# Two transfers of destination rows per visit in place of five, in a two-layer graph network on one Trainium2 core

## What is computed

```python
# layer 0
q, k, v = feat @ Wq.T + bq, feat @ Wk.T + bk, feat @ Wv.T + bv      # (n, 8, 32)
score = clip(einsum('ehd,ehd->eh', q[edge_dst], k[edge_src]) / sqrt(32), -10, 10)
alpha = softmax of score over the edges of one destination
wv = segment_sum(alpha * v[edge_src], edge_dst)
x = feat + wv @ Wp.T + bp;  x = x + gelu(layernorm(x) @ W1.T + b1) @ W2.T + b2
# layer 1
z = leaky_relu((feature @ W_s.T)[src] + (feature @ W_t.T)[dst], 0.2)
e = z @ W_attn.T;  alpha = softmax of e over the edges of one source
out = segment_sum(feature[src] * alpha, dst) @ W_fc.T + b_fc
# each layer is followed by x = layernorm(x + layer(x))
```

## Time and profile before

| | us |
|---|---|
| median of the three runs | 4053.36 |
| the profiled execution, its time | 4052.72 |
| the profiled execution, its span | 4050.9 |
| pass 0 (attention of layer 0) | from 155 to 1560 |
| feed-forward part and projections | 1560 to 1950 |
| pass 1 (scores of layer 1) | 1950 to 3215 |
| softmax sums | 3215 to 3370 |
| third pass (sums of layer 1) | 3370 to 4050 |

### The profile page before, as it was taken

One profiled execution on the slowest core, in us unless ns is written; L12 is line 12 of the kernel. 1 busy time (PEld: TensorE's weight loads), 2 busy tenths in 40 slices (PEclk: granted clock), 3 DMA queues, 4 the chain that ended last, 5 costly groups with the idle time before them and its releaser, 6 DMA issues. The chain is left out here.

```text
span 4050.9 us, 56408 instructions
## 1 busy us (share of the span) xinstructions
PE 2350.9 (58%) x11454; PEld 1705.1 (42%) x11455; DVE 2223.8 (55%) x6089; ACT 1218.1 (30%) x3239; POOL 1941.0 (48%) x1970
## 2 busy tenths in 40 slices
PE   4666666666666665887333333333333396777776
PEld 2344444444444444675122222222222195566555
DVE  5565565555555563334344444444444596677675
ACT  0255555555555553333122222222222200111111
POOL 0255555555555552212655656655555303444443
PEclk9888888888888887898565666666666656888998
DMA  4666665665666662113667677666766605666664
GB/s 140 196 175 176 176 177 174 180 181 169 177 178 179 176 182 84 65 63 100 207 205 205 206 210 209 200 202 203 205 200 200 181 0 164 200 205 198 193 208 148
DMA packets 365706, 698.61 MB, mean 172 GB/s; under 512 B 77317, under 2 KB 247039, under 8 KB 365674
## 3 DMA queue, kind: packets, MB, share of 16 engines
q0 software_dynamic: 134784, 425.63, 36.1%
q1 hardware_dynamic: 220602, 256.40, 20.2%
q10 hardware_dynamic: 10288, 16.23, 1.1%
HBM read 597.23 MB, written 100.85 MB: 172 GB/s over the span
## 5 line engine op out<-in xcount | busy, mean ns | idle before, releaser
L878 PE MATMUL ps_px<-sb_parts,sb_bits 128*128 x4860 | 886.7, 344 | 902.9 <-DVEq L1590 362.3
L759 POOL DMA_INDIRECT sb_ring<-kv_rows,sb_idx x810 | 792.3, 978 | 723.8 <-DVE sb_msg L1458 377.5
L878 PEld LDWEIGHTS ps_px<-sb_parts,sb_bits 128*128 128x128 bf16 x4860 | 566.5, 121 | 1238.4 <-DVEq L1590 586.7
L888 PE MATMUL ps_pa<-sb_msg,sb_onehot 128*128 128x264 f32 x1620 | 567.5, 483 | 433.1 <-DVE sb_msg L1458 349.0
L1125 ACT ACTIVATE sb_bits<-sb_bits 128x256 bf16<-128x256 bf16 x810 | 322.7, 409 | 1019.2 <-remote 725.9
L1443 DVE TENSOR_TENSOR sb_prod<-ps_px,sb_ring 128x512 f32<-128x512 f32 x405 | 278.7, 688 | 573.7 <-remote 339.9
L888 PEld LDWEIGHTS ps_pa<-sb_msg,sb_onehot 128*128 128x128 f32 x1620 | 345.0, 235 | 551.3 <-DVE sb_msg L1458 373.6
L759 POOL DMA_INDIRECT sb_ring<-proj_rows,sb_idx x324 | 311.7, 962 | 321.8 <-issue 156.1
L759 POOL DMA_INDIRECT sb_w<-narrow_rows,sb_idx x324 | 310.1, 957 | 207.4 <-DVEq L1590 113.0
L759 POOL DMA_INDIRECT sb_w<-feat_rows,sb_idx x162 | 158.6, 979 | 426.1 <-issue 190.3
L1593 DVE SCALAR_TENSOR_TENSOR sb_prod<-sb_msg,sb_attn_hi 128x256 f32<-128x256 f32 x810 | 300.5, 421 | 0.7 <-issue 0.7
(11 more groups left out here) (242 smaller groups left out, 3070.2 us busy)
## 6 DMA issues: line engine op xcount, KB each, us to landing
sb_bits<-dst_short SPq DMA_DIRECT2D x280, 192.0 KB
x_edges<-sb_ring SPq DMA_DIRECT2D x54, 768.0 KB
sb_slots<-x_edges SPq DMA_DIRECT2D x54, 768.0 KB
x_edges<-sb_slots SPq DMA_DIRECT2D x27, 768.0 KB
sb_w<-x_edges SPq DMA_DIRECT2D x27, 768.0 KB
sb_msg<-lo_rows SPq DMA_DIRECT2D x28, 576.0 KB
sb_ring<-kv_rows,sb_idx POOLq DMA_INDIRECT x810
kv_rows<-sb_slots ACTq DMA_DIRECT2D x25, 256.0 KB, 2.8
```

What stands on the lines that cost most here:

```text
L759: pool.indirect_dma_start(out=out[:, i, :], out_offset=None, in_=rows, in_offset=bass.IndirectOffsetOnAxis(ap=idx[:, 2 * p + i:2 * p + i + ...
L878: mm = pe.matmul(px[:, j, 0:width], onehot_t[:, j, :], flat(visit_parts[:, bass.ds(parity, 1), a, 0:width]), start=(a == 0), stop=(a == 2))
L888: mm = pe.matmul(pa[:, 0:C + H], onehot[:, j, :], msg[:, j, :], start=(p == 0 and i == 0), stop=True, skip_group_check=True)
```

## The change

The destinations of a visit come in two transfers: halves 0 to 2 in one of 4608 bytes per partition, halves 3 and 4 in one of 3072 bytes. The first is issued after ACT has read half 2, the second after half 4. Each has its own semaphore; ACT waits for the first before halves 0 to 2 and for the second before halves 3 and 4. `node_parts` loads the whole rows of 774 bf16 elements (1548 bytes), also in pass 0, in both passes as one contiguous run per node.

```diff
-        drow_in = [[sem(f"drow_in{L}_{h}") for h in range(HALVES)] for L in range(2)]
+        drow_in = [[sem(f"drow_in{L}_{g}") for g in range(2)] for L in range(2)]
...
+        ROW_HALVES = [[0, 1, 2], [3, 4]]
...
-                width = CW if L else C
...
-                def rows(tile, h):
-                    sp.dma_start(drow[:, h].rearrange("p j e -> p (j e)"),
-                                 dst_short[bass.ds(tile + h * R, R), :].rearrange("j e -> (j e)").partition_broadcast(P)).then_inc(drow_in[L][h], 16)
+                def rows(tile, g):
+                    h, n = ROW_HALVES[g][0], len(ROW_HALVES[g])
+                    sp.dma_start(drow[:, h:h + n].rearrange("p h j e -> p (h j e)"),
+                                 dst_short[bass.ds(tile + h * R, n * R), :].rearrange("j e -> (j e)").partition_broadcast(P)).then_inc(drow_in[L][g], 16)
 
                 def node_parts(node, parity):
-                    sp.dma_start(visit_parts[:, bass.ds(parity, 1), :, 0:width].rearrange("p o a c -> p (o a) c"),
-                                 part_rows[bass.ds(node, P), :, 0:width]).then_inc(node_in[L], 16)
+                    sp.dma_start(visit_parts[:, bass.ds(parity, 1)].rearrange("p o a c -> p (o a c)"),
+                                 part_rows[bass.ds(node, P)].rearrange("n a c -> n (a c)")).then_inc(node_in[L], 16)
...
-                for h in range(HALVES):
-                    rows(tile, h)
+                for g in range(2):
+                    rows(tile, g)
                 for c in range(THIRDS):
                     indices(tile, c)
...
                         sp.wait_ge(far[L], v * HALVES + h + 2)
                         sp.sem_inc(sp_seen, 1)
-                        rows(after, h)
+                        for g in range(2):
+                            if h == ROW_HALVES[g][-1]:
+                                rows(after, g)
...
-                act.wait_ge(drow_in[L][h], v * 16 + 16)
+                act.wait_ge(drow_in[L][h >= ROW_HALVES[1][0]], v * 16 + 16)
```

More of the change, by code:

```diff
@@ L588, in run @@
                         sp.sem_inc(sp_seen, 1)
-                    for h in range(HALVES):
-                        sp.wait_ge(drow_in[L][h], total * 16 + 16)
+                    for g in range(2):
+                        sp.wait_ge(drow_in[L][g], total * 16 + 16)
                         sp.sem_inc(sp_seen, 1)
```

## The result

The changed kernel takes 4010.35 us (median of five runs, 4004.60 to 4019.04), the kernel before, run beside it, 4053.36 us. The ratio is 0.9893, with a 95% interval from 0.9868 to 0.9918: 43 us less, where 20 were forecast. The profiled executions differ by 42.4 us (4050.9 and 4008.5), and the place of each first and last gather tells where.

A forecast was written before the change was run, and what follows sets the result against it. Waits, not a busy engine, were taken to bound passes 0 and 1, with SP's late index loads in pass 1. Against 4052.72 us, -21 + 7 - 1.6 - 4 = -19.6 gave 4033 us, range 3995 to 4072.

The forecast's parts named there:

- The pause at the first gather: Pass 1, POOL's wait for indices at a visit's start: 1.0 us shorter per visit, from 6.3 to about 5.3 us.
- In 21 visits: Pass 1: the 1.0 us gain counted in 21 visits, 21 us; at most 48 us, at least nothing.
- nothing for the other index loads: Pass 1: removing half 3's load ahead of the second index load, needed for pair 5, is worth nothing; no wait shows.
- a different rhythm of stalls: Pass 1: a stall fewer or more per visit, 4 to 6 us x 26, would upset the forecast altogether.
- The give-back: Pass 1: a third of the gain lost to a longer pause before pair 9, +7 us; between 0 and all 21.
- The seam: Between pass 0 and pass 1: three load issues fewer on SP while POOL stands idle, -1.6 us.
- Packets: Pass 0: fewer and larger packets on the load queue, -4 us, bound 9 us; pass 1: 0.
- Bursts and later loads: Both passes: bunched loads cost 0 (bad end +40 us in pass 1); ACT's waits for later-issued loads stay hidden.
- B: Rival: nothing moves, 4050 us; what SP gains at pair 0 in pass 1 is lost at pair 9; chance 0.20.
- C: Rival: pass 1's first pause falls to that of pair 9, indices issued in loaded time, about 4000 us; chance 0.15.
- D: Rival: bunched loads delay the first gathers after each pause, +40 us over 26 visits, about 4086 us; chance 0.15.
- E: Rival: pass 1's node_parts already went as 128 packets, so only pass 0's cut counts; already in the sum, no own chance.

The follow-up runs named there:

- Experiment 6: The changed kernel with eight semaphore increments that nothing waits for, put on SP ahead of each visit's first index load in pass 1: 4029.38 us, ratio 0.9933.
- Experiment 8: The changed kernel with pass 1's node_parts load issued behind the first index load, the two transfers of destinations behind the second and third: 3995.84 us, ratio 0.9849.
- parts_whole: The kernel before with node_parts loading whole rows in pass 0 as well, the five transfers of destinations kept: 4047.32 us, ratio 0.9986.
- five_late_3: The kernel before with its five 192 KB transfers issued where the changed kernel issues its two (three after half 2, two after half 4): 4014.86 us, ratio 0.9914.
- pass1_only: The kernel before with the change made in pass 1 alone, pass 0 loading as before: 3344.91 us, ratio 0.9989, in a 3344 us session.
- small_slots: The changed kernel with 32 KB row loads after halves 0 and 1, 512 KB after half 2: 1.0006 and 1.0005 in 3344 us sessions, 0.9961 in a slow one.

## Why the prediction was right and wrong

The direction, the place and the range were right. The size was less than half of what came (20 us of 43), by two terms of the sum in pass 1.

**The pause at the first gather, 1.0 us shorter: nearly right.** Forecast were 0.6 us from SP's issue and 0.4 us from the bytes. Measured are 0.69 us (4.28 to 3.59, last gather to issue) and 0.58 us (3.25 to 2.67, issue to start, 0.52 of them in the load's own packets). The forecast pause was 5.3 us; it is 4.97, where it was 6.36.

**"In 21 visits", and nothing for the other index loads: this step failed.** I multiplied a shorter pause by an unchanged number of pauses at the first gather, 21 us, with 48 as the upper bound. There the number fell to 9 and the sum by 98.7 us (147.7 - 49.0). But I had also set the load ahead of the second index load at nothing, since no wait for it showed. After the change POOL waits 15 times, 57.3 us, for the second and third index load, before it 2 times, 7.9 us. All three loads together, the waits over 2 us fell from 153.9 us in 26 to 101.0 us in 24: 53 us, by their length and not by their number. Experiment 6 shows that 0.3 us on SP's queue move the number at the first gather by about ten. I had named "a different rhythm of stalls" as what would upset the forecast, and gave it no term.

**The give-back, a third: failed too, in size and in kind.** It is 63 of 99 us, the other pauses' growth from 134.4 to 197.2. I had DVE a pair behind and a longer pause before pair 9; there the pauses fell from 21 to 8. Of the 63 us, 49 are the waits for the second and third index load, 5 are waits over 2 us for slots (102.8 to 108.1), and the rest is in pauses under 2 us. The net is 36 us, forecast 14. Experiment 8, in which each load of rows is issued right behind an index load, is without most of these waits and takes 19.5 us less in pass 1.

**The seam, -1.6 us: not seen.** It is 353.8 and 354.3 us in the two, and 351.6 in `parts_whole`, which has all eight issues there; what differs from run to run is larger than the term.

**Packets, -4 us in pass 0: the size was off.** Measured are 7.5 us, near the bound of 9, and all of it from `node_parts`. My way to it, engine time per byte, was wrong or at least unproven, since that time hardly changed.

**Bursts and later loads, 0: nothing speaks against it.** ACT waits for no load of destinations in pass 1, and `five_late_3` and the changed kernel, the one with five small and the other with two large transfers at the same places, have pass 1 within 7.2 us of one another. The size of the packets is tested by that; the bunching, which both have, is not tested by itself.

**The rivals.** B, nothing moves, is out. C had the pause fall to that of pair 9, and gave 4000 us; the time comes near to it, but not by its way, since where there is a pause it is still 5 us. Its argument, SP's instructions being so slow in the loaded time that a few fewer are worth much, is what seems to have been weighed too low: eight marks ahead of the index load cost 18 to 21 us. D is out: the 40 us did not come, and packets of 4608 and 3072 bytes do no worse in pass 1 (1257.4 us) than packets of 1536 bytes at the same places (1264.6). The Trainium skill's rule that a DMA engine turns between queues at whole packets ("DMA: Bandwidth & Descriptors", section Queues, rings and completion order) is neither shown nor refuted by that; a harm from it does not show here. E was as told: in the body of pass 1 `node_parts` was already whole.

The 2.67 us from the issue of a 5 KB load to POOL's start contain 0.44 us of packets; the other 2.2 us are not packets (before the change 3.25 less 0.96, 2.3 us). The Trainium skill (same page, section Anatomy of one DMA) has about 2.0 us fixed, and has it for DMAs that GpSimd issues, not for every DMA as the prediction says. These loads, which SP issues, agree with it in size. The 2.2 us are paid on the path only by the loads that are issued late.

## What to carry to other kernels

Where an engine that issues DMAs runs a queue of mixed loads, the load that somebody is about to wait for belongs first, and the others behind it; how many transfers the others are matters less. Before multiplying a shorter wait by its count, ask where the engine will wait next: here most of the waits for the first index load went over to the second and the third, which were hardly waited for before, and a few tenths of a microsecond on the queue changed where the pauses fall. And where a wait has two conditions that come together, time it against the issue and the packets of each instead of trusting the one that the profile names.

## What was not expected of the hardware

**Two speeds of the same program.** The kernel before took 4053 to 4065 us in some sessions and 3343 to 3345 us in others, and nothing in between. Windows of `pass1_only` at 3345 us, pass 0 and pass 1:

```profile
160.00:1300.00 1140.00, 822.21 (x4205) 567.69 (x4206) 818.90 (x1761) 717.79 (x2215) 784.39 (x803) 0.93 0.74 216
1670.00:2670.00 1000.00, 512.71 (x2362) 299.48 (x2360) 605.74 (x2363) 286.09 (x524) 760.16 (x788) 0.62 0.86 259
```

Against the earlier trace rows the engines do the same work; in pass 1 the clock is the same 0.62, and the DMA engines are busy 86% of the time in place of 69%. The other engines don't come to a stop: in pass 1 the longest wait of ACT is 6.7 us and that of DVE 4.4 us, in the kernel before at 4053 us 15.7 and 13.1 us. SP's instructions that only control differ too; whether they are the cause or another sign of it is not shown. The marks at L524 (L526 in `pass1_only`), over 400 us of pass 1, first at 4053 us, then at 3345 us (ns, least, median, most):

```profile
L524 SPq EVENT_SEMAPHORE  x203: 3/17/733, 2206.0 to 2600.0; - x102
```

```profile
L526 SPq EVENT_SEMAPHORE  x248: 17/17/17, 1904.8 to 2291.5; - x124
```

None of 248 takes over 17 ns in the one. In the other 53 of 203 take over 600 ns, some 40 times the median, as those that stand in the loaded time of the earlier trace rows do. At 3345 us SP has time to spare and waits for the gathers to land, which it does nowhere in pass 1 at 4053 us:

```profile
SPq L526 <- DMA sb_ring<-proj_rows,sb_idx: 328.0, 133, 7.3
SPq L526 <- DMA sb_slots<-proj_rows,sb_idx: 300.5, 78, 8.8
SPq L526 <- DMA sb_w<-narrow_rows,sb_idx: 75.4, 34, 3.9
```

What decides between the two is open. It is not the chip as such, since one chip showed both, and no kernel here made it come or go. The changed kernel as it stands was run only in the sessions at 4053 to 4065 us. In the others ran the change in pass 1 alone and `small_slots`, which has the whole node rows in both passes and all but two tiles of the large transfers; both are worth nothing there.

**A few control instructions can be worth 0.5%** in the sessions at 4053 to 4065 us: eight increments per visit, 216 in all, cost 18 to 21 us of pass 1 by one trace against three, a tenth of a microsecond each, although nothing waits for one of them.
